# Context spectra of odd frequencies from paired rows, rows summed by a transfer, and rotated loop bodies on five engines

## What is computed

```python
# first block, query = layernorm(x), memory = ctx
s = sigmoid(norm(query)); ten times: s = 3.9 * s * (1 - s)
q = query * (1 + 0.1 * (s - 0.5)) * position
Q, K, V = q @ Wq.T + bq, mem @ Wk.T + bk, mem @ Wv.T + bv
Qf, Kf, Vf = fft(Q), fft(K), fft(V)              # over the 512 tokens
QKV = hamilton(hamilton(Qf * filt, Kf * filt), Vf * filt)
x = x + ifft(QKV).real
# second block
tokens = layernorm(layernorm(x)) with gamma and beta
top1 = argmax(tokens @ gate.T); out = x + layernorm(x) + weight * expert[top1](tokens)
```

## Time and profile before

| | |
|---|---|
| runs | 3343.62 us median of 3 (3343.38 to 3343.95) |
| profiled execution | 3342.41 us, of which the span is 3340.6 us |
| busy in the span | PE 3237.0, VectorE (DVE) 2799.1, ScalarE (ACT) 2238.1, POOL 1300.1 us |
| PE in 40 slices | 6999999999999999999999679999999999999998 |
| DVE in 40 slices | 4999999999999999999999767777777777777774 |
| POOL in 40 slices | 3456757666666667576665500000000000000001 |
| granted clock of TensorE, mean | 0.987 |

### The profile page before, as it was taken

One profiled execution on the slowest core, in us unless ns is written; L12 is line 12 of the kernel. 1 busy time (PEld: TensorE's weight loads), 2 busy tenths in 40 slices (PEclk: granted clock), 3 DMA queues, 4 the chain that ended last, 5 costly groups with the idle time before them and its releaser, 6 DMA issues. The chain is left out here.

```text
span 3340.6 us, 54951 instructions
## 1 busy us (share of the span) xinstructions
PE 3237.0 (97%) x17944; PEld 2682.9 (80%) x17944; DVE 2799.1 (84%) x3891; ACT 2238.1 (67%) x4836; POOL 1300.1 (39%) x1608
## 2 busy tenths in 40 slices
PE   6999999999999999999999679999999999999998
PEld 5777777777777777777777369999999999999997
DVE  4999999999999999999999767777777777777774
ACT  5666666676766666666766367777777777777764
POOL 3456757666666667576665500000000000000001
PEclk9999999999999999999999789999999999999999
DMA  6432221222121222312130233333444343333431
GB/s 229 153 101 79 74 92 61 78 76 88 63 88 63 88 76 65 111 52 88 64 102 26 83 108 115 114 118 123 127 127 122 120 127 114 113 105 116 124 102 38
DMA packets 299918, 327.15 MB, mean 98 GB/s; under 512 B 47600, under 2 KB 179056, under 8 KB 299760
## 3 DMA queue, kind: packets, MB, share of 16 engines
q1 hardware_dynamic: 284400, 308.12, 29.0%
q0 software_dynamic: 15360, 16.99, 1.5%
HBM read 256.96 MB, written 101.97 MB: 107 GB/s over the span
## 5 line engine op out<-in xcount | busy, mean ns | idle before, releaser
L1424 POOL TENSOR_TENSOR tally<-tally,unit 1x1 f32<-1x1 f32 x16 | 8.4, 524 | 1286.0 <-DVE res L1871 1286.0
L1527 PE MATMUL out_ps<-wo_h,act_h 128*128 128x512 f32 x1024 | 403.3, 394 | 0.0
L1528 PE MATMUL out_ps<-wo_h,act_l 128*128 128x512 f32 x1024 | 403.0, 394 | 0.0
L1529 PE MATMUL out_ps<-wo_l,act_h 128*128 128x512 f32 x1024 | 398.5, 389 | 0.0
L1860 DVE TENSOR_TENSOR act_l<-act,act_h 128x512 fp32r<-128x512 f32 x256 | 176.5, 690 | 264.6 <-ACT act_h L1694 264.6
L1830 DVE TENSOR_TENSOR wi_l<-w_sum,wi_h 128x1024 fp32r<-128x1024 f32 x128 | 156.8, 1225 | 114.4 <-ACT wi_h L1626 113.3
L1468 PE MATMUL y_bank<-tok_h,wi_h 128*128 128x256 f32 x768 | 221.8, 289 | 5.4 <-DVE tok_l L1796 5.4
L1529 PEld LDWEIGHTS out_ps<-wo_l,act_h 128*128 128x128 f32 x1024 | 192.4, 188 | 43.0
L508 PE MATMUL pair<-w_qh,q_high 128*128 128x512 f32 x512 | 222.1, 434 | 1.5 <-ACT q_low L740 1.5
L1468 PE MATMUL y_bank<-tok_h,wi_l 128*128 128x256 f32 x768 | 217.7, 284 | 0.0
L1468 PE MATMUL y_bank<-tok_l,wi_h 128*128 128x256 f32 x768 | 217.5, 283 | 0.0
(11 more groups left out here) (244 smaller groups left out, 10924.9 us busy)
## 6 DMA issues: line engine op xcount, KB each, us to landing
w_raw<-in_L_ffn_wi SPq DMA_DIRECT2D x256, 256.0 KB, 2.9
w_raw<-in_L_ffn_wo SPq DMA_DIRECT2D x128, 512.0 KB, 4.8
w_raw<-in_x SPq DMA_DIRECT2D x32, 1024.0 KB, 5.3
w_raw<-in_ctx SPq DMA_DIRECT2D x32, 1024.0 KB, 5.3
x_res<-in_x SPq DMA_DIRECT2D x31, 1024.0 KB
out<-x_res SPq DMA_DIRECT2D x31, 1024.0 KB
slots<-rows SPq DMA_DIRECT2D x4, 4160.0 KB, 15.7
got<-slots SPq DMA_DIRECT2D x15, 1040.0 KB, 7.8
```

The costliest lines, as they stand in the source:

```text
L1424: nc.gpsimd.tensor_tensor(tally[:], tally[:], unit[:], ALU.add).then_inc(tallied, 1)
L1527: nc.tensor.matmul(out_ps[t][:], ah, oh, start=(j == 0 and h == 0), stop=False)
L1528: nc.tensor.matmul(out_ps[t][:], al, oh, start=False, stop=False)
L1529: last = nc.tensor.matmul(out_ps[t][:], ah, ol, start=False, stop=(j == STEPS - 1 and h == 1))
```

## The change

1. The context's odd frequencies. With the difference d of rows n and n + 256, a cosine column takes rows n and 256 - n with opposite signs, and a sine column takes them with the same sign. So VectorE forms one paired block of 128 rows for the cosines and one for the sines (the row 0 of each block stands for a row without a partner), and each needs a matmul of 128 columns in place of 256. Queries keep the old form.
2. The inputs for that. The rows 128 to 255 and 384 to 511 are also wanted backwards: the host passes a copy of the context's rows in that order (`ctx_back`). SP loads rows 0 to 255 (`c_low_rows`), the third block, and the two backward blocks, one of them to a new buffer `c_back`. POOL's queue then adds rows 256 to 511 of DRAM onto the first two blocks with one accumulating transfer (`add_rows`), after a one-element instruction.
3. `folds_c` becomes six instructions of 512 elements a partition.
4. ScalarE's row sums use one scratch tile in place of two, and each waits for the one before.
5. The bodies of all five engines are written in a new order.

```diff
+def forward_paired():
+    m = forward_odd().reshape(128, 2, 256)
+    sine = m[:, 0, 128:].copy()
+    sine[0] = m[0, 1, 128:]
+    return sine
...
+    c_pair = nc.inline_tensor(np.outer(np.arange(P) > 0, [-1, 1]).astype(np.float32), "c_pair").ap()
...
 # SP
+                    def context_rows(b):
+                        every = seq(ctx_in, b)
+                        sp.dma_start(c_in[:, 0:2], every[:, 0:2]).then_inc(c_low_rows, 16)
+                        sp.dma_start(c_in[:, 2], every[:, 2]).then_inc(c_loaded, 16)
+                        back = ctx_back[bass.ds(b, 1)].rearrange("a t p n -> p (a t) n")
+                        sp.dma_start(c_in[:, 3], back[:, 0]).then_inc(c_loaded, 16)
+                        sp.dma_start(c_back[:], back[:, 1]).then_inc(c_loaded, 16)
...
                     def body(b):
+                        real_store(b - 4)
+                        load_c(b)
                         real_spread(b - 3)
-                        store(b - 5)
-                        load_res(b - 4)
-                        load_x(b - 1)
+                        store(b - 4)
+                        load_x(b)
                         real_gather(b - 3)
-                        load_c(b)
                         real_out(b - 2)
-                        real_store(b - 3)
+                        load_res(b - 3)
...
 # TensorE, dft
                         for t in range(2):
+                            if w == 0:
+                                last = nc.tensor.matmul(ps[:, 256 + t * P:256 + (t + 1) * P], folded[:, 1, t, u * P:(u + 1) * P],
+                                                        fwd_p[:] if t else fwd_o[:, 0, 0:P], start=False, stop=True,
+                                                        skip_group_check=True)
+                                continue
...
 # ScalarE
-                        if t > 1:
-                            act.wait_ge(sums, b * SUMS + t - 1)
-                        nc.scalar.activation(unused[t % 2][:], src[:, t, 0:DIM], ACT.Copy,
+                        if t > 0:
+                            act.wait_ge(sums, b * SUMS + t)
+                        nc.scalar.activation(unused[:], src[:, t, 0:DIM], ACT.Copy,
...
 # POOL
+                    def add_rows(b):
+                        pool.wait_ge(c_low_rows, b * 16 + 16)
+                        wait(pool, c_ticked, b)
+                        tv(c_tick[:], k["one"][0:1, 0:1], k["one"][0:1, 0:1], ALU.mult).then_inc(c_ticked, 1)
+                        nc.gpsimd.dma_start(c_in[:, 0:2], seq(ctx_in, b)[:, 2:4], accum_op=ALU.add).then_inc(c_summed, 16)
...
                     def body(b, p):
-                        scales1(b - 1)
-                        scatter(b - 5, 1 - p)
-                        real_bins(b - 2)
+                        add_rows(b)
                         mean1(b)
                         stats1(b)
                         mean2(b - 3)
                         start1(b)
                         stats2(b - 3, 1 - p)
+                        scales1(b)
+                        real_bins(b - 2)
+                        scatter(b - 4, p)
...
 # VectorE
-                            fold(b, c_in, c_fold, cf_ready, (c_loaded, b * 16 + 16), b * 8 - 4)
-                            fold_again(b, c_in, c_fold, cf_ready)
+                            dve.wait_ge(c_loaded, b * C_LOADS + C_LOADS)
+                            dve.wait_ge(c_summed, b * 16 + 16)
+                            v.scalar_tensor_tensor(c_in[:, 2], c_in[:, 2], -2.0, c_in[:, 0], ALU.mult, ALU.add).then_inc(cf_ready, 1)
+                            v.tensor_tensor(c_in[:, 3], c_in[:, 3], c_back[:], ALU.subtract).then_inc(cf_ready, 1)
+                            wait(dve, f1_mm, b * 8 - 4)
+                            v.tensor_tensor(c_fold[:, 0, 0], c_in[:, 0], c_in[:, 1], ALU.add).then_inc(cf_ready, 1)
+                            v.tensor_tensor(c_fold[:, 0, 1], c_in[:, 0], c_in[:, 1], ALU.subtract).then_inc(cf_ready, 1)
+                            dve.wait_ge(cf_ready, b * FOLDS_C + 2)
+                            v.scalar_tensor_tensor(c_fold[:, 1, 0], c_in[:, 3], paired[:, 0:1], c_in[:, 2], ALU.mult, ALU.add).then_inc(cf_ready, 1)
+                            v.scalar_tensor_tensor(c_fold[:, 1, 1], c_in[:, 2], paired[:, 1:2], c_in[:, 3], ALU.mult, ALU.add).then_inc(cf_ready, 1)
```

227 lines of the change are left out of this document (118 added, 109 removed).

## The result

| | before | after |
| --- | --- | --- |
| median of the runs, us | 3343.8 (3343.4 to 3344.1) | 3388.6 (3387.5 to 3393.6) |
| profiled execution's span, us | 3340.6 | 3387.0 |
| ratio, 95% interval | | 1.0138 [1.0125, 1.0151] |

The forecast was 3320 with a range of 3297 to 3350: wrong in sign and outside the range.

What follows compares the result with a forecast made beforehand. TensorE sets the 57.52 us period with VectorE 1.3 us behind; after the change VectorE sets 56.46. Sum: 3342.4 - 33 + 9.5 for the ends = 3319, with 1.2 for the median 3320 us, range 3297 to 3350.

Steps and rivals of the forecast that it cites:

- I cost their moves at nothing, as each is still separated from its producer by other matmuls.: TensorE: ranks, inverses and logits are moved, not added, so their new places cost nothing.
- -1.74 us: TensorE, context's odd transforms: 128 columns instead of 256 save 4 x 0.43 = 1.74 us per sequence.
- By that VectorE, not TensorE, sets the new pace.: Steady period: VectorE at 56.5 us bounds it, against 55.8 for TensorE alone.
- What VectorE pays to POOL, 1.0 us, bounds 0 and 2.3: VectorE beside POOL's real frequencies: contention adds 1.0 us to each period, bounds 0 and 2.3.
- the floor of 55.46: VectorE's period without its waits and without what it pays to POOL: 57.52 - 1.31 - 0.75 = 55.46 us.
- the 10 to 15 of the forecast: POOL's real frequencies: expected to start without a wait of 10 us and take 10 to 15 us.
- POOL holding VectorE for its whole instruction: Rival, shared SBUF ports: VectorE blocked for POOL's whole instruction, period 58.3 us, total 3378; chance 0.02.
- ScalarE's sixteen sums ... are costed at nothing: ScalarE's serialised sums: no cost, ScalarE busy 1160 of 1740 us; without cover, a few tenths per period on TensorE.
- The ends, +2.5 and +7.: Start: added transfers delay the first mean 2.5 us; end of stage one: last real frequencies push scatter 29 by 7.
- the -33 of the forecast: Steady sequences: a gain of 1.06 us in each of 31 intervals, 33 us.
- TensorE stays the bound: Rival: VectorE needs only 55.5 us, TensorE sets a period of 55.8, total 3299; chance 0.17.
- POOL's loop: Rival: contended real frequencies make POOL's loop set the period, likely 58 to 59 us, 3368 to 3399; chance 0.10.

Runs made afterwards that it cites:

- e3: The change's new order on all engines with the old context arithmetic (no paired rows, no accumulating transfer): 3432.7 us, ratio 1.0264.
- e17: e1 with two scratch tiles shared by both streams of ScalarE's sums and ScalarE's loop written out: 3344.1 us, ratio 0.9998.
- e10: e1 with 1.3 us of VectorE's context fold work left out of every sequence but the first: 3364.1 us, ratio 1.0062.
- e9: e6 with the ranks' matmuls moved on TensorE behind the context's first two eye removals: 3319.7 us, ratio 0.9933.
- e18: e9 with two scratch tiles shared by both streams of ScalarE's sums and ScalarE's loop written out: 3304.3 us, ratio 0.9879.
- e1: The change with ScalarE's loop edge moved back ahead of the context's third high copy, instruction order unchanged: 3365.3 us, ratio 1.0065.
- e5: e4 with POOL issuing the accumulating transfer behind the scatter instead of behind stats2: 3356.0 us, ratio 1.0038.
- e16: e1 with ScalarE's sums of x put behind the query copies for the second sequence alone: 3357.4 us, ratio 1.0039.
- e4: The change's new context arithmetic in the old order on all engines, accumulating transfer issued by POOL behind stats2: 3456.5 us, ratio 1.0338.
- e6: e5 with the load of pos issued ahead of the first context's loads: 3352.6 us, ratio 1.0026.
- e13: The kernel before the change, with only the ranks' matmuls moved behind the first two eye removals: 3344.4 us, ratio 1.0001.
- e2: The change with ScalarE's row sums and squares of x put behind the last query low copy, as before: 3577.8 us, ratio 1.0697.
- e14: e1 with two scratch tiles shared alternately by both streams of ScalarE's sums, loop kept: 3401.2 us, ratio 1.0167.

## Why the prediction was wrong, step by step

**"I cost their moves at nothing, as each is still separated from its producer by other matmuls."** This is the step that failed first. e3 has the moves without the arithmetic: 59.1 against 57.56, 1.6 us a sequence, 48 over the program, as much as the paired rows give. Not all of it is the moves': e3 keeps the one scratch tile, and two tiles give back 0.6 (e17), so about 1.0 is left for them. The traces show how. TensorE's waits for ScalarE's copies were 8.7 us in 28 sequences and are 12.0 + 11.4 + 6.6, about 0.7 more in each; the 6.6 are the part that goes with faster sums. And three of four inverses used to stand between two removals; two of the three now stand between a removal and a transform. Before, the inverse with its next removal took 482.18 - 480.23 = 1.95:

```profile
480.23 1.88 PE L542 MATMUL even_ps<-r_spec,inv 128*128 128x512 f32 x4
...
481.55 0.80 PE L485 MATMUL xt_ps<-c_high,minus_eye 128*128 128x512 f32 x1
...
482.18 0.61 PE L470 MATMUL xt_ps<-fwd_e,q_fold 128*128 128x128 f32 x4
```

After, the removal takes 0.41 and the inverse 1.72, 2.13 together:

```profile
966.05 0.58 PE L516 MATMUL xt_ps<-q_high,minus_eye 128*128 128x512 f32 x1
...
966.46 1.88 PE L573 MATMUL even_ps<-r_spec,inv 128*128 128x512 f32 x4
...
968.18 0.61 PE L496 MATMUL xt_ps<-fwd_e,q_fold 128*128 128x128 f32 x4
```

Twice 0.2 and the 0.7 of waits make 1.1 of the 1.6. The whole account, each instruction counted up to the start of the next, in four short sequences of e3 against before: inverses +2.0 (5.25 became 7.2), context removals +0.6, turns +0.1, query removals -0.5, projections -0.4, context transforms -0.2. How much an inverse takes by this count goes with its neighbour: 1.31 ahead of a removal or a projection, 1.72 ahead of a transform or a turn.

**"-1.74 us" for the context's transforms:** right, 59.1 - 57.5 = 1.6.

**"By that VectorE, not TensorE, sets the new pace."** Wrong for the change as it stands (e10): TensorE with its waits sets 57.45. Once ScalarE's sums are faster it is right, at 56.9 (e17). In the old order 56.65 was reached when the ranks were moved (e9: 3319.7; that this is the forecast's 3320 is luck, it is another order). Nor was 56.5 VectorE's floor in every order: e18 runs at 56.05.

**What VectorE pays to POOL, 1.0 us, bounds 0 and 2.3:** about right in size. From 600 to 1200 us VectorE is busy 587.50 us in e1 and 595.67 in e17, which makes 56.3 and 56.5 a sequence; in the old order with the same arithmetic 590.33 (e9) and 596.67 (e18), 55.8 both. Against the floor of 55.46 that is 0.8 to 1.0 in the new order and 0.3 in the old. The real frequencies take 11.6 us, within the 10 to 15 of the forecast. What the sum left out are short gaps between VectorE's instructions: e17's period is 0.4 above its busy time. The rival of POOL holding VectorE for its whole instruction gave 58.3 us; that did not happen. By the rule of the Trainium skill, page "SBUF — State Buffer", section "SBUF: two separate sides", a VectorE instruction with two inputs in SBUF would be blocked to the end of POOL's whenever POOL starts first. The traces speak against that price here: in e17, where VectorE does set the pace, the period is 56.9 and not 58.3. In e1, at 57.45, VectorE is idle 1.2 us of it, and taking 1.3 us from VectorE changes nothing (e10).

**"ScalarE's sixteen sums ... are costed at nothing"**, with the remark that without cover it would be "a few tenths per period". The remark was the truth: 0.6 (e17 against e1), 17 us over the program. The order itself takes the cover away, and that stood in the text.

**The ends, +2.5 and +7.** The transfers and `pos` cost less than the 2.5, within the bounds of 0 and 5: e5's first projection is 1.3 late and its sequence 2 on time. What was missed is the order: +14.6 with it (after, e3), nothing without (e5). The sums between the query's copies have nothing beside them on TensorE before the first inverse; e16 gives 3 us for one sequence. e1, with the same lists as the change, starts 5.6 us earlier than it (+9.0 against +14.6), but that is the fastest of e1's four executions (3359.1, the others 3363.6 to 3368.4), and e10, in e1's order, has +14.1. The granted clock has a part in that; from 40 to 60 us, the change and then e1:

```profile
40.00:50.00 10.00, 6.20 (x23) 3.74 (x22) 2.29 (x1) 9.59 (x24) 1.08 (x4) 0.82 1.06 389
50.00:60.00 10.00, 9.22 (x33) 7.35 (x33) 7.29 (x7) 4.89 (x7) 5.48 (x7) 0.67 0.15 53
```

```profile
40.00:50.00 10.00, 5.65 (x21) 3.90 (x20) 0.29 (x1) 9.08 (x22) 1.98 (x6) 0.83 1.06 387
50.00:60.00 10.00, 10.00 (x54) 8.53 (x53) 8.63 (x9) 7.54 (x16) 4.58 (x5) 1.00 0.11 37
```

Both are idle for some 4 us of the first ten (before the change TensorE was busy 8.76 there, at 1.00); the change then ran on at 0.67, which is 3.3 us of work undone. Why one and not the other I can't say, and the rest of the start stays open. The tail, +10.8, is +7.4 for the order (e3) and +3.4 for the arithmetic (e5): above the forecast's 7, and partly by its way: behind sequence 31's first projection the last `add_odd` starts after 93.6 us instead of 87.5, 6.1 later.

**Not in the forecast at all: ScalarE's loop edge.** 23 us (e1). The change moved the place at which ScalarE's list jumps back. No rival had it, and the trace of before had no hint of it: ScalarE's copy behind the old edge waits 0.43 us for TensorE in every sequence, inside the loop and outside it.

The middle in one line: -1.6 x 31 for the arithmetic, +1.6 x 31 for the order with the one scratch tile, +23 for the edge, against the 21.0 that were measured and the -33 of the forecast.

**The rivals.** "TensorE stays the bound" named the right engine at 3299, with the order's price at zero. The rival on the other side, POOL's loop, is not what happened (432 us of waiting before the means), but e4 shows that a loop through POOL can set the period: one step at another place of its list, and it is 61.3.

## What to carry to other kernels

When an order written by hand is changed on several engines, cost the order by itself: what stands between a copy's request and its use on both engines, and run the order with the old arithmetic, since gain and loss of one size hide each other. Where two engines are both nearly full, an edit on one shows nothing until the hand-over between them is mended too (e6 +8, e13 +0.5, together -24): judge edits in pairs there. And look where each engine's loop jumps back: where its instructions are brought in again in each pass (the instruction rows of the DMA list), begin the loop at another place, or where the engine waits at the edge itself (e2), or write it out, and measure.

## What the runs showed of the hardware

- A loop edge can cost ScalarE a gap that no semaphore explains: 1.8 to 2.2 us in the change, 3.4 to 5.3 in e14, none in e1 and none where the loop is written out (e17, e18). The gaps come with instruction packets in every pass, 50 and 49 from 400 to 1500 us against 2 in e1. The same place of the edge was free in e1 and not in e14, which differs from it in two scratch tiles and their waits; both wait about 4 us for a projection two copies ahead, so a wait nearby doesn't cover the gap. A wait at the edge itself did in e2 (44 packets, 2.17 us for TensorE in every sequence, no gap).
- TensorE's granted clock fell behind short idle time too, and not every time: in e5 behind a wait of 0.83 us in one sequence and not behind one of 0.88 in the sequence before. Where it fell it cost more than the wait: transforms of 0.23 us took 0.42, and in e14 the clock was 0.59 for 6 us behind ScalarE's gap of 4.1.
- In the change an accumulating transfer of 512 KB takes POOL 0.8 to 1.5 us to issue, median 1.0, and a median of 7.3 us to land. Its place in POOL's list alone makes 100 us of 3450 (e5 against e4).
- What a matmul takes up to the start of the next goes with its neighbour: 1.31 us for the four instructions of 128x512 of an inverse ahead of a removal, 1.72 ahead of a transform (before and e3).
